# Local attention: the copy of the first key product goes ahead of the second quarter's exponentials on ScalarE

## The reference

```
x = x + 0.5 * ffn0(layernorm(x))      # experts and a shared gated layer
x = x + gla(layernorm(x))             # chunked gated linear attention
x = x + 0.5 * ffn0(layernorm(x))
x = x + 0.5 * l1ffn(layernorm(x))     # ternary weights, relu
x = x + local_attention(layernorm(x))
x = x + 0.5 * l1ffn(layernorm(x))
```

```
q, k, v = split(x @ w_qkv.T + b_qkv)
scores  = q . k[window] / sqrt(16)
attn    = softmax(scores)
out     = (attn . v[window]) @ w_out.T + b_out
```

## Time and profile before

| what | value |
|---|---|
| median of 3 runs | 1665.37 us (1662.6 to 1667.76) |
| the profiled execution's own time | 1673.61 us |
| its span | 1671.5 us, 42410 instructions |
| PE busy | 1609.6 us, 96% |
| DVE busy | 1180.0 us, 71% |
| ACT busy | 873.3 us, 52% |
| POOL busy | 706.9 us, 42% |
| local attention, first product to last context | about 1326 to 1545 us of the span |

### The profile page before, as it was taken

The page is one execution under the profiler, slowest core; times in us unless marked ns, Lnnn a source line. Parts: engine busy times, 40 slices in busy tenths (PEclk is TensorE's granted clock), DMA queues, the critical chain, the costliest instruction groups (busy, mean ns, idle before and its releaser), DMA issues.

```text
span 1671.5 us, 42410 instructions
## 1 busy us (share of the span) xinstructions
PE 1609.6 (96%) x15094; PEld 1083.9 (65%) x15095; DVE 1180.0 (71%) x2536; ACT 873.3 (52%) x1507; POOL 706.9 (42%) x660
## 2 busy tenths in 40 slices
PE   6999999999999999999999999999999989998998
PEld 3665556666666776766555656666666767777666
DVE  6677775666666666667865556666689678888786
ACT  5354443444366666654333334444376576775674
POOL 2342232343235455442332323334245467777342
PEclk9999999999999999999999999999999999999999
DMA  7132223333311211003210123333432033131011
GB/s 259 51 101 86 86 89 92 110 110 110 89 39 26 38 25 25 0 1 99 89 39 29 38 74 99 111 110 104 102 63 50 2 78 79 53 67 41 14 38 51
DMA packets 91303, 115.71 MB, mean 69 GB/s; under 512 B 9424, under 2 KB 76528, under 8 KB 91184
## 3 DMA queue, kind: packets, MB, share of 16 engines
q1 hardware_dynamic: 70832, 71.17, 15.2%
q0 software_dynamic: 20352, 42.88, 9.0%
HBM read 66.11 MB, written 47.90 MB: 68 GB/s over the span
## 4 chain that ended last, share of the span: by engine, by line
PE 80%; DVE 7%; ACT 5%; issue 3%; POOL 2%; another core or an unknown queue 2%; DMA 1%; DVEq 0%; SPq 0%; ACTq 0%; POOLq 0%
PE ps L1890 18%; PE ps L1892 17%; PE ps L1891 17%; PE ps L2169 3%; PE ps L2170 3%; PE ps L2129 3%; PE ps L2130 3%; PE ps L1906 2%; PE ps L2101 2%; PE ps L2082 2%; PE ps L2265 1%; PE ps L2434 1%; PE ps L2400 1%; PE ps L2412 1%
## 5 line engine op out<-in xcount | busy, mean ns | idle before, releaser
L753 POOL DMA_INDIRECT routed<-work x142 | 136.1, 959 | 235.3 <-DVE work L1590 230.2
L1890 PE MATMUL ps<-later_hi,work 128*128 (+1 forms) x632 | 203.1, 321 | 0.3 <-DVE work L1570 0.2
L1892 PE MATMUL ps<-later_hi,work 128*128 (+1 forms) x632 | 203.0, 321 | 0.0
L1891 PE MATMUL ps<-later_lo,work 128*128 (+1 forms) x632 | 203.0, 321 | 0.0
L1890 PE MATMUL ps<-xt_hi,wsh 128*128 128x512 f16 x508 | 192.7, 379 | 8.2 <-DVE work L1463 7.1
L1892 PE MATMUL ps<-xt_hi,wsh 128*128 128x512 f16 x508 | 192.5, 379 | 0.0
L1891 PE MATMUL ps<-xt_lo,wsh 128*128 128x512 f16 x508 | 192.5, 379 | 0.0
L926 ACT ACTIVATE work<-ps 128x512 f32<-128x512 f32 x128 | 76.4, 597 | 178.2 <-PE ps L1892 171.6
L1463 DVE SCALAR_TENSOR_TENSOR work<-ps,work 128x512 f32<-128x512 f32 x128 | 88.0, 688 | 76.8 <-ACT work L926 66.3
L1890 PE MATMUL ps<-wsh,work 128*128 128x256 f16 x512 | 139.7, 273 | 1.1 <-DVE work L1389 0.6
L1892 PE MATMUL ps<-wsh,work 128*128 128x256 f16 x512 | 139.7, 273 | 0.4 <-issue 0.4
(11 more groups left out here) (266 smaller groups left out, 4306.3 us busy)
## 6 DMA issues: line engine op xcount, KB each, us to landing
work<-expert_x SPq DMA_DIRECT2D x142, 129.0 KB
yg<-in_w_later SPq DMA_DIRECT2D x9, 496.0 KB
w1q<-in_w_later SPq DMA_DIRECT2D x9, 496.0 KB
yg<-in_w SPq DMA_DIRECT2D x16, 256.0 KB
values<-wsh SPq DMA_DIRECT2D x8, 512.0 KB, 4.2
later_hi<-values SPq DMA_DIRECT2D x16, 256.0 KB, 5.0
later_lo<-values SPq DMA_DIRECT2D x16, 256.0 KB, 5.1
out_x<-x SPq DMA_DIRECT2D x8, 512.0 KB, 3.0
```

The lines of the kernel that those rows point to most:

```text
L753: nc.gpsimd.indirect_dma_start(routed[:, :], bass.IndirectOffsetOnAxis(m.homes[:, i:i + 1], 0), m.t_y[:, i % 4, :], None).then_inc(s[f"til ...
L1890: nc.tensor.matmul(out_, a[0], b[0], start=start, stop=False)
L1891: nc.tensor.matmul(out_, a[0], b[1], start=False, stop=False)
L1892: return nc.tensor.matmul(out_, a[1], b[0], start=False, stop=stop)
```

## The change

In quarter 1 of steps 0 to 6 ACT copies product j = 2 before `exps(g, 1)` instead of after it; copy j = 3 stays behind the exponentials. Quarters 0, 2 and 3 keep their order, only written with another condition. The test for the last step falls away because that step has returned before. No other engine's program is touched.

```diff
@@ -1185,12 +1185,15 @@
                             turned(g2, t2)
                         if has_turn(g, t, 3):
                             ct_hi(*turns_back(g, u, t, 3))
+                        if t == 1:
+                            queries_keys(g + 1, 1 - u, (KT,))
                         exps(g, t)
-                        if not is_last(g):
-                            if t < 2:
-                                queries_keys(g + 1, 1 - u, (2 * t, 2 * t + 1))
-                            elif t == 2:
-                                values_rows(g + 1)
+                        if t == 0:
+                            queries_keys(g + 1, 1 - u, range(KT))
+                        elif t == 1:
+                            queries_keys(g + 1, 1 - u, (KT + 1,))
+                        elif t == 2:
+                            values_rows(g + 1)
```

## The result

Over nine runs each the changed kernel took 1659.49 us (1656.55 to 1662.6) and the kernel before 1663.84 (1660.93 to 1667.76). The ratio is 0.9973 with a 95% interval of 0.9963 to 0.9983: about 4.4 us, where 3.9 were forecast. Timed again later it was 0.9976 (0.9964 to 0.9988). That is within the 0.3% named as the bound, and clear of no change.

The account below looks back on a forecast made before the run. PE bounds the kernel, with 80% of the chain, so only ended PE idle time pays. 3.0 us from steps 1 to 6 plus 0.9 from step 0 give 3.9, taken off 1665.37: 1661.5 us, range 1658.0 to 1665.6.

Parts of the forecast that it names:

- the 0.3% named as the bound: Whole kernel: a change within 0.3%, 5.0 us, can hardly be told from none; the forecast lay below it.
- The wait on the moved copy: Steps 1 to 6: the transposes' wait for key copy j = 2 goes entirely, 0.50 us in step 2, 3.0 in all.
- the sum: Whole kernel: 3.0 us from steps 1 to 6 plus 0.9 from step 0 give 3.9, so 1661.5 us.
- What is late next: After the transposes: xt_hi, xt_lo, sums and POOL's normalize move 0.50 us too; margins 0.07 at xt_hi, 0.09 at POOL.
- The first rival: At xt_hi the gain stops and PE waits for POOL at turn(g, 1): gain 1.5 us, time 1663.9, chance 0.12.
- The delayed exponentials: Quarter 1's exponentials end 0.6 to 0.7 us later, about 2.8 us before sums(g, 1) needs them: cost nothing.
- The slower rival: At sums(g, 1) DVE waits for the exponentials, 0.69 us in seven steps, 4.8 us: time 1670.2, chance 0.05.
- Step 0: Transposes gain 1.16 us, the chain to POOL 0.88; gives 0.9 us, and idle before the turn grows 1.08 to 1.36.
- The clock: Behind step 0's 2.73 us wait a half-clock spell may come, go or move: about 1 us either way, outside the sum.
- the 1 us either way of the range: Range allowance for a clock drop coming or going behind step 0's 2.73 us wait, worth about 1 us.
- PE's instruction supply: Score gaps, 1.4 us in all, keep their places; rival: they move, 2.6 us comes back, 1664.1 us, chance 0.06.
- The sign that it named: Attention's stretch: the prediction is wrong if it is shorter by less than 2 us or more than 6.

Follow-up runs that it names:

- both copies ahead: Against the kernel before, key copies j = 2 and j = 3 both precede the exponentials of quarter 1: 1.0039; with value gathers cut 0.9987.
- the added ACT instruction: One more copy into a scratch tile ahead of copy j = 3: on the changed kernel 1.0024, on the kernel before 1.0003, both against the kernel before.
- the two slowed orders: Both key copies ahead of quarter 1's exponentials, 1.0039, and the changed kernel with one more ACT copy before copy j = 3, 1.0024, against the kernel before.

## Why the prediction was right

*The wait on the moved copy.* The distance of 0.72 became 0.22 in all six steps, and the row is gone. A gap-free step gained 0.55, not 0.50: the next turn now starts 0.87 us behind the start of the eight transposes, where it started 0.93 behind it after the wait (the rows are 1.04 and 1.09 long), a term that the sum left out. Six steps give 3.3 instead of 3.0.

*What is late next.* Each link of the chain through xt_hi, xt_lo, sums and POOL moved, and the margin at turn(g, 1) stayed below 0.1. The first rival (the gain stops at xt_hi) did not happen, but it was a hair away: both copies ahead and the added ACT instruction made it happen, with turns waiting 0.48 and 0.25 for POOL.

*The delayed exponentials.* Their cost was nothing, as said; with the exponentials delayed by a further 2.6 us the steps were as short. The slower rival is out.

*Step 0.* Turn(0, 1) came 0.96 us earlier, 0.88 were forecast. The copies and the exponentials overlap by 0.10 to 0.14 in the new order, where the prediction reckoned with 0.09 and 0.10, so ACT reached xt_hi a little sooner. The wait before the turn fell to 0.80 and did not grow to 1.36: since PE meets a short wait for POOL earlier in the step now (0.28, before turn(0, 0), which starts 1.34 behind the transposes instead of 0.91), it lost 0.4 of its lead there. That sub-step was wrong, and nothing hung on it.

*The clock.* The spell of 0.50 behind PE's 2.7 us of idle time was there in both kernels and wandered between executions of one. The granted clock stands ahead of the last two columns; these are the changed kernel's first and second execution, from 4.5 and from 3.2 us behind the start of turn(0, 2), which starts at 1350.50 and 1353.78:

```profile
1355.00:1356.00 1.00, 1.00 (x4) 0.15 (x1) 0.00 (x0) 0.02 (x1) 0.65 (x1) 0.50 0.00 0
```

```profile
1357.00:1358.00 1.00, 1.00 (x5) 0.39 (x4) 0.50 (x2) 1.00 (x2) 1.00 (x2) 0.91 0.20 28
```

The first was low until 1356.5, 6.0 us behind the turn, the second until 1357.2, 3.4 behind it; its step 0 to 1 was 1.2 us shorter (26.02 against 27.26). That is the 1 us either way of the range, and more than a fourth of the gain in a single trace. In both traces with both key copies ahead the clock stayed full behind a wait of 2.73, and from the start of turn(0, 2) to the next transposes they took 11.9 us, against 12.9 and 14.15 in the two of the changed kernel.

The Trainium skill ("TensorE: Matmul & The Clock Gate", Part 1) says that the point of switching varies between runs, by half a microsecond either way. The traces agree that it varies; here by 2.6 us, and in some the spell is missing.

*PE's instruction supply.* The prediction had the gaps keep their places. In PE's program they did; but which of the steps had one differed from one execution of the same kernel to the next. It also priced them by their idle rows: the three of 1.4 us in all lengthened the steps by 2.2. They neither came nor went with the change in a way that two traces of each kernel show, and with the gathers cut the gain stayed. Whether they are neutral to the order of ACT in general is doubtful: the two slowed orders had 4.9 and 5.8 us of them in one trace each, the changed kernel up to 4.2, but both copies ahead cost 10.5 us over the changed kernel in the timings with full gathers and 4.0 with short ones.

*The sign that it named.* An attention shorter by less than 2 us or by more than 6 was to show it wrong. The first pair of traces gives 5.2, the second 1.3. That test failed by the second pair without the mechanism failing: with gaps that change by 3 us from one execution to the next, the difference of two stretches could not decide it.

*The sum.* 3.3 from six steps and 0.96 from step 0 are 4.3 us by the traces; 4.4 and 4.0 were measured, with an uncertainty near 2 each, and 3.9 were forecast. The mechanism was right and both terms were a little small.

## What to carry to other kernels

When an instruction moves ahead of another on an in-order engine, follow what the released engine meets next, link by link, and write down each margin: here ACT's 0.07 and POOL's 0.09 us decided whether 0.5 us a step was kept or given back, and one copy more moved ahead lost it all. Read a small gain off the steps that nothing else disturbs, in more than one execution of both kernels; the difference of two whole spans was 14.2 us where the change was worth 4.4.

## What the runs showed of the hardware beyond that

PE's unexplained idle times in the attention were tied to the gathers of values by DMA: 1.0 to 5.8 us in traces with full gathers, 0 to 0.4 in the three with gathers cut to an eighth. Those in the scores of steps 2 to 6 lay behind the same matmuls in every trace with full gathers, and the one with 0.66 us of idle time cost 0.89. A slower ACT order was slower by more than its chain (by some 6.5 us with both copies ahead, by some 4 with an added copy), and for the first the excess vanished with the gathers. The half-clock spell behind the same 2.74 us wait ended 2.6 us later in one execution than in another of the same kernel, and cost 1.2 us more; in both traces with both copies ahead no spell followed a wait of 2.73.
